# The first expert layer: one quad of tokens dense, three quads routed to their experts' blocks

## What is computed

```python
# layer 0: causal attention, 16 heads of 128, then
scores = sigmoid(x @ gate_w)                      # 32 experts
w, i = top_k(scores, 6); w /= w.sum() + 1e-20
g = einsum('td,edf->tef', x, wg); u = einsum('td,edf->tef', x, wu)   # 96 hidden values each
out = einsum('tef,efd,te->td', silu(g) * u, wd, combine(w, i)) \
      + (silu(x @ sg) * (x @ su)) @ sd            # shared: 192 hidden values
# layer 1: state-space layer (8 heads of 64, conv of 4 taps, dt = softplus, gated norm), then
# 16 experts of 176 hidden values, top 4 within 2 of 4 groups, and a shared part of 352
```

## Time and profile before

| | us |
|---|---|
| median of 3 runs | 1666.55 |
| lowest and highest run | 1663.94, 1666.93 |
| span of the profiled execution | 1664.1 |
| TensorE busy | 1607.4 |
| DVE, ACT, GpSimd busy | 1131.1, 764.6, 628.7 |
| bytes moved by DMA | 277.75 MB |

### The profile page before, as it was taken

The page is one execution under the profiler, slowest core; times in us unless marked ns, Lnnn a source line. Parts: engine busy times, 40 slices in busy tenths (PEclk is TensorE's granted clock), DMA queues, the critical chain, the costliest instruction groups (busy, mean ns, idle before and its releaser), DMA issues.

```text
span 1664.1 us, 29632 instructions
## 1 busy us (share of the span) xinstructions
PE 1607.4 (97%) x9944; PEld 1403.7 (84%) x9944; DVE 1131.1 (68%) x2877; ACT 764.6 (46%) x1889; POOL 628.7 (38%) x379
## 2 busy tenths in 40 slices
PE   7999999999999979999999999999999999999997
PEld 6988888898888868888888888888888888888886
DVE  5878878787887765556467568748784867753533
ACT  5666656666665543434433443325333533323221
POOL 2322223232222004323377335841575147533242
PEclk9999999999999999999999999999999999999999
DMA  6444335343443016666676556655655466555563
GB/s 212 159 140 143 141 118 180 132 158 139 142 141 137 1 59 205 191 196 205 199 225 188 184 176 209 194 187 165 207 189 175 146 206 197 178 175 172 195 206 107
DMA packets 101241, 277.75 MB, mean 167 GB/s; under 512 B 13488, under 2 KB 17584, under 8 KB 100112
## 3 DMA queue, kind: packets, MB, share of 16 engines
q1 hardware_dynamic: 101136, 276.39, 51.6%
HBM read 229.18 MB, written 46.63 MB: 166 GB/s over the span
## 4 chain that ended last, share of the span: by engine, by line
PE 60%; issue 14%; DVE 13%; POOL 6%; ACT 4%; DMA 1%; SPq 1%; POOLq 0%; DVEq 0%; ACTq 0%
PE psum L352 54%; POOL act_sb L578 4%; PE psum L1324 2%; DVE s_sb L1019 1%; PE psum L1335 1%; PE psum L1514 1%; POOL mix L600 1%; ACT p_sb L701 1%; PE psum L1314 1%; ACT kT_hi L660 1%; DVE s_sb L1017 1%; DVE kT_lo L913 1%; DVE pT_lo L1034 1%; DVE x L934 1%; DVE p_sb L1027 1%
## 5 line engine op out<-in xcount | busy, mean ns | idle before, releaser
L352 PE MATMUL psum<-xT_hi,gu_w 128*128 128x512 f32 x1616 | 550.3, 401 | 4.2 <-DVE act_sb L1082 4.0
L578 POOL TENSOR_TENSOR act_sb<-act_sb,comb 128x512 f32<-128x512 f32 x184 | 311.1, 1691 | 614.8 <-DVE act_sb L1082 614.6
L1082 DVE TENSOR_TENSOR act_sb<-psum,gated 128x512 f32<-128x512 f32 x204 | 140.7, 690 | 378.9 <-PE psum L352 372.6
L742 ACT ACTIVATE gated<-psum 128x512 f32<-128x512 f32 x204 | 122.2, 599 | 600.3 <-PE psum L352 597.8
L352 PEld LDWEIGHTS psum<-xT_hi,gu_w 128*128 128x128 f32 x1616 | 304.2, 188 | 78.0 <-DVE act_sb L1082 5.6
L352 PE MATMUL psum<-xT_lo,gu_w 128*128 128x512 f32 x808 | 319.6, 395 | 0.0
L352 PEld LDWEIGHTS psum<-d_w,act_hi 128*128 128x128 f32 x1632 | 221.5, 188 | 19.7 <-issue 2.1
L544 POOL TENSOR_TENSOR split_stage<-raw_stage,split_stage 128x768 fp32r<-128x768 f32 x56 | 103.1, 1840 | 354.2 <-ACT split_stage L650 354.2
L352 PE MATMUL psum<-d_w,act_hi 128*128 128x256 f32 x1632 | 227.7, 282 | 0.4 <-ACT act_hi L750 0.4
L352 PEld LDWEIGHTS psum<-xT_lo,gu_w 128*128 128x128 f32 x808 | 152.2, 188 | 28.8
L1088 DVE TENSOR_TENSOR act_lo<-act_sb,act_hi 128x512 fp32r<-128x512 f32 x204 | 148.8, 729 | 2.1 <-ACT act_hi L750 1.8
(11 more groups left out here) (203 smaller groups left out, 3473.6 us busy)
## 6 DMA issues: line engine op xcount, KB each, us to landing
gu_w<-w_split SPq DMA_DIRECT2D x204, 512.0 KB, 3.6
d_w<-w_split SPq DMA_DIRECT2D x204, 256.0 KB, 3.8
w_split<-split_stage SPq DMA_DIRECT2D x56, 768.0 KB, 3.9
raw_stage<-w_all SPq DMA_DIRECT2D x56, 384.0 KB, 4.3
decay_all<-decay_dram SPq DMA_DIRECT2D x32, 384.0 KB, 5.3
in_w<-w_split SPq DMA_DIRECT2D x40, 256.0 KB, 4.1
aw_raw<-attn_w SPq DMA_DIRECT2D x8, 1024.0 KB, 6.3
comb<-l_comb_dram SPq DMA_DIRECT2D x128, 64.0 KB, 3.1
```

The source lines that it names most:

```text
L352: last = nc.tensor.matmul(out_ap, w, m, start=start and n == 0, stop=stop and n == len(pairs) - 1, **kw)
L578: pool.tensor_tensor(act_sb[:, s % 2, :], act_sb[:, s % 2, :], comb[:, comb_block(s) % 2, :], ALU.mult).then_inc(comb_done, 1)
L742: act.activation(gated[to, s % 2, :], psum[0:to.stop - to.start, G_BANK, :], ACT.Silu).then_inc(gated_ready, 1)
L1082: dve.tensor_tensor(act_sb[r, s % 2, :], psum[r, G_BANK if packed(s) else U_BANK, :], gated[r, s % 2, :], ALU.mult).then_inc(t_ready, 1)
```

## The change

Layer 0 is dense for quad 0 alone. Quads 1 to 3 keep their two shared tiles, and each of their tokens goes to its six experts only.

- While quad 0 is computed, the gates of quads 1 to 3 are made (`choice_logits`, `choose`), a prefix sum by matmul gives each (token, choice) its row in its expert's region of `xs` in DRAM (`rank`, `rows_placed`), and GpSimd scatters the token rows there by indirect DMA: 36 units of two DMAs of 128 rows, one unit a tick, each after the one before has landed. `xs` is filled with zeros before, during attention (`zero`, 42 stores).
- A table gives the first row of each of 103 blocks of 128 rows (`table`, `rows_read`); SP reads these numbers into registers and loads, per block, the 128 rows and the weights of the block's expert (`rows_load`, `weights_load`).
- Then 103 block ticks: transposes, gate and up, SiLU, product, down, all in plain f32 without splitting, and a store to `os` for every second block.
- In layer 1's steps GpSimd gathers the six results of each token (36 units), and DVE adds them with their weights (`combine_rows`).
- All engines walk a list of ticks instead of steps: 32 dense ticks, 8 pauses, 103 blocks, 104 dense ticks. The 52 slots of a pair are mapped to ticks by `MARKS`: pair 0 lies over the blocks, pairs 1 to 3 lie in layer 1's steps, slots 0 to 44 in 9, 19 and 19 ticks, slots 44 to 52 in two.
- The norms of quads 1 and 2 move into the last attention group, that of quad 3 to tick 2.

```diff
+def tiles_of(f, q):
+    return f["lead"] if f is L0 and q else f["tiles"]
+STEP_LIST = [(f, q, j) for f in LAYERS for q in range(QUADS) for j in range(tiles_of(f, q))]
...
+SLOT = L0["experts"]
+TOP = L0["top"]
+WIDTH = L0["width"]
+BLOCK = 128
+BLOCK_BITS = 7
+REGION = ROUTED_TILES * P
+BLOCKS = (REGION * TOP + SLOT * (BLOCK - 1)) // BLOCK
+SPARE = BLOCKS - REGION * TOP // BLOCK
+LAST_ROW = SLOT * REGION + (SPARE - 1) * BLOCK
+UP = 2 * WIDTH
+BW = DC * UP + D
+ZERO_ROWS = 1280
+ZEROED = 6
+XS_ROWS = ZERO_ROWS * ZEROED * (GROUPS - 1)
+assert LAST_ROW + BLOCK <= XS_ROWS and BLOCKS <= P
+XB_RING, BW_RING, OUT_RING = 4, 6, 4
...
+Tick = namedtuple("Tick", "gate high down block")
+BREAK = first_step(L0, QUADS - 1)
+PAUSES = 8
+def dense_ticks(a, b):
+    at = lambda s: s if a <= s < b else None
+    return [Tick(at(s), at(s - 1), at(s - LAG), None) for s in range(a, b + LAG)]
+TICKS = dense_ticks(0, BREAK) + [Tick(None, None, None, None)] * PAUSES + [Tick(None, None, None, n) for n in range(BLOCKS)] \
+    + dense_ticks(BREAK, STEPS)
+B0 = BREAK + LAG + PAUSES
+K0 = B0 + BLOCKS
+def tick_of(s):
+    return s if s < BREAK else K0 + s - BREAK
+CHOICE = {1: 0, 2: 3, 3: 6}
+COUNTED = CHOICE[3] + 4
+WEIGHED = {1: 14, 2: 17, 3: 20}
+PAIRS_OF = QUAD * TOP // 2
+SCATTERED = 4
+UNITS_IN = 4
+GATHERED = [K0 + u for u in range(20)] + [K0 + 24 + u for u in range(4)] + [K0 + 29 + u for u in range(8)] + [K0 + 44 + u for u in range(4)]
+COMBINED = 3
...
+NORM = -6
+MARKS = (((NORM, 28), (0, 33), (4, 37), (8, 39), (9, B0 + 1), (52, B0 + 92)),
+         ((NORM, K0 + 15), (-3, K0 + 17), (0, K0 + 18), (44, K0 + 27), (52, K0 + 29)),
+         ((NORM, K0 + 30), (0, K0 + 33), (44, K0 + 52), (52, K0 + 54)),
+         ((NORM, K0 + 55), (0, K0 + 58), (44, K0 + 77), (52, K0 + 79)))
+SLOTS_AT = {}
+for _p in range(PAIRS):
+    for (_v, _n), (_w, _m) in zip(MARKS[_p], MARKS[_p][1:]):
+        for _s in range(_v, _w):
...
+            def zero(n):
+                by_part = xs.rearrange("(n p r) d -> n p (r d)", p=P, r=ZERO_ROWS // P)
+                dst = by_part[n] if isinstance(n, int) else by_part[bass.ds(n, 1)].rearrange("a p w -> p (a w)")
+                sp.dma_start(dst.rearrange("p (a w) -> p a w", w=BANK), zeros[:].to_broadcast([P, ZERO_ROWS // P * D // BANK, BANK])) \
+                    .then_inc(xs_zeroed, 16)
...
+            def weights_load(n):
+                row = first_row_of(n)
+                if n == 0:
+                    sp.wait_ge(down_done, BREAK)
+                wait(sp, b_down_done, n - BW_RING + 1)
+                sp.dma_start(block_w(n), l0_w[bass.ds(region_of(row), 1)].rearrange("a p w -> p (a w)")).then_inc(w_loaded[n % BW_RING], 16)
+            def rows_load(n):
+                row = first_row_of(n)
+                if n == 0:
+                    for q in ROUTED_QUADS:
+                        sp.wait_ge(scattered[q], 16 * QUAD * TOP)
+                wait(sp, xb_turned, n - XB_RING + 1)
+                sp.dma_start(xb[:, n % XB_RING, :], xs[bass.ds(row, BLOCK)]).then_inc(tokens_loaded[n % XB_RING], 16)
+            def block_store(n):
+                i, pair = n % 2, n // 2
+                if i == 0 and n < BLOCKS - 1:
+                    return
+                a = n - i
+                sp.wait_ge(b_copied, n + 1)
+                sp.dma_start(os[a * BLOCK:(n + 1) * BLOCK].rearrange("(i p) d -> p i d", p=P),
+                             b_out[:, 2 * (pair % 2):2 * (pair % 2) + i + 1, :]).then_inc(b_stored[pair % 2], 16)
...
+            for i, t in enumerate(TICKS):
+                s = t.gate
+                if t.block is not None:
+                    n = t.block
+                    if n + XB_RING < BLOCKS:
+                        rows_load(n + XB_RING)
+                    if n + BW_RING - 1 < BLOCKS:
+                        weights_load(n + BW_RING - 1)
+                    if n >= 1:
+                        block_store(n - 1)
+                if i == K0 - 1:
+                    gu_load(BREAK)
+                    gu_load(BREAK + 1)
+                    block_store(BLOCKS - 1)
...
+            def scatter(u):
+                q, v = ROUTED_QUADS[u // PAIRS_OF], u % PAIRS_OF
+                if u == 0:
+                    pool.wait_ge(xs_zeroed, 16 * ZEROED * (GROUPS - 1))
+                else:
+                    pool.wait_ge(scattered[ROUTED_QUADS[(u - 1) // PAIRS_OF]], 32 * ((u - 1) % PAIRS_OF + 1))
+                if v == 0:
+                    pool.wait_ge(placed, ROUTED_QUADS.index(q) + 1)
+                tile, ks = unit_rows(u)
+                for k in ks:
+                    pool.indirect_dma_start(xs, bass.IndirectOffsetOnAxis(ap=row_of[:, tile, k:k + 1], axis=0), x[:, FIRST_TILE + tile, :], None) \
+                        .then_inc(scattered[q], 16)
+            def gather(u):
+                if u == 0:
+                    blocks_stored(pool)
+                    pool.wait_ge(weighed, len(ROUTED_QUADS))
+                else:
+                    pool.wait_ge(og_loaded[(u - 1) % UNITS_IN], 32 * ((u - 1) // UNITS_IN + 1))
+                wait(pool, combined, u - UNITS_IN + 1)
+                tile, ks = unit_rows(u)
+                for j, k in enumerate(ks):
+                    pool.indirect_dma_start(og[:, u % UNITS_IN, j, :], None, os, bass.IndirectOffsetOnAxis(ap=back_of[:, tile, k:k + 1], axis=0)) \
+                        .then_inc(og_loaded[u % UNITS_IN], 16)
...
+            for i, t in enumerate(TICKS):
+                if t.gate is not None and not shared(t.gate):
+                    combine(t.gate)
+                if 0 <= i - SCATTERED < len(ROUTED_QUADS) * PAIRS_OF:
+                    scatter(i - SCATTERED)
+                if t.gate == 4:
                     ssm_constants()
-                if s == 9:
+                if t.gate == 9:
                     out_low()
-                for p in range(PAIRS):
-                    o = s - FRONT[p]
+                if i in GATHERED:
+                    gather(GATHERED.index(i))
...
+            def block_turned(n):
+                act.wait_ge(xb_turned, n + 1)
+                if n >= 2:
+                    act.wait_ge(gu_ready, n - 1)
+                act.activation(xbT[:, n % 2].rearrange("p c t -> p (c t)"), psum[:, TURN_BANK, 0:DC * BLOCK], ACT.Copy).then_inc(xbT_ready, 1)
+            def block_gate(n):
+                h = slice(0, WIDTH)
+                act.wait_ge(gu_ready, n + 1)
+                wait(act, bt_ready, n - 1)
+                act.activation(b_gated[h, n % 2, :], psum[h, gu_bank(n), 0:P], ACT.Silu).then_inc(b_gated_ready, 1)
+            def block_copy(n):
+                act.wait_ge(b_down_done, n + 1)
+                pair, i = n // 2, n % 2
+                if i == 0:
+                    wait(act, b_stored[pair % 2], 16 * (pair // 2))
+                act.activation(b_out[:, 2 * (pair % 2) + i, :], psum[:, DOWN_BANK, 0:D], ACT.Copy).then_inc(b_copied, 1)
...
+                    if norm and i in (12, 16):
+                        q = i // 4 - 2
+                        ln_stats(q, o_added, (GROUPS - 1) * 2 * PAIRS + 2 * q + 2)
+                        ln_root(q)
+                    if norm and i in (13, 17):
+                        ln_rows(0, i // 4 - 2)
...
+            def combine_rows(u):
+                tile, ks = unit_rows(u)
+                to = x[:, FIRST_TILE + tile, :]
+                dve.wait_ge(og_loaded[u % UNITS_IN], 32 * (u // UNITS_IN + 1))
+                for j, k in enumerate(ks):
+                    ins = dve.scalar_tensor_tensor(to, og[:, u % UNITS_IN, j, :], mix_of[:, tile, k:k + 1], to, ALU.mult, ALU.add)
+                    if j == 0:
+                        chained(ins)
+                ins.then_inc(combined, 1)
...
+            def block_act(n):
+                h = slice(0, WIDTH)
+                dve.wait_ge(b_gated_ready, n + 1)
+                wait(dve, b_down_done, n - 1)
+                dve.tensor_tensor(b_act[h, n % 2, :], psum[h, gu_bank(n), P:2 * P], b_gated[h, n % 2, :], ALU.mult).then_inc(bt_ready, 1)
...
+            def block_turn(n):
+                pe.wait_ge(tokens_loaded[n % XB_RING], 16 * (n // XB_RING) + 32)
+                wait(pe, xbT_ready, n)
+                for c in range(DC):
+                    last = pe.transpose(psum[:, TURN_BANK, c * BLOCK:(c + 1) * BLOCK], xb[:, n % XB_RING, c * P:(c + 1) * P], ident[:])
+                last.then_inc(xb_turned, 1)
+            def block_gate_up(n):
+                pe.wait_ge(xbT_ready, n + 1)
+                pe.wait_ge(w_loaded[n % BW_RING], w_landed(n % BW_RING, n, BREAK))
+                wait(pe, bt_ready, n - 1)
+                w, h = block_w(n), slice(0, WIDTH)
+                for i in range(2):
+                    last = chain(psum[h, gu_bank(n), i * P:(i + 1) * P],
+                                 [(w[:, c * UP + i * WIDTH:c * UP + (i + 1) * WIDTH], xbT[:, n % 2, c, :]) for c in range(DC)])
+                last.then_inc(gu_ready, 1)
+            def block_down(n):
```

(35 more changed lines are left out.)

579 lines of the change are left out of this document (414 added, 165 removed).

## The result

The changed kernel takes 1848.84 us (median of 4 runs, 1844.14 to 1851.56), the kernel before beside it 1665.24 us (4 runs, 1663.86 to 1666.93). The ratio is 1.1095, 95% interval 1.1074 to 1.1117. The forecast was 1692.5 us, with a range up to 1800: the direction was right, the size was not, and the result lies outside the range. The profiled execution's span is 1849.8 us, 185.7 us more than before.

The account below looks back on a forecast made before the run. TensorE, busy 97%, was taken to bound the kernel; its 127 us saved would be given back in waits. 620 + 188 + 227 + 643 + 12 = 1690, so 1692.5 us against 1666.55; range 1605 to 1800, the forecast's own 1650 to 1740.

Parts of the forecast that it names:

- Stage A: Attention and its tail: two more layer norms add 9 us, zero stores 0; dense steps start at 620 us.
- Stage B: Quad 0 dense while 72 indirect stores scatter: GpSimd sets the pace, 4.6 us a unit, 188 us in all.
- Rival 2: Indirect DMA costs a full GpSimd instruction, 6.5 us a unit in scatters, gather ticks +36: 1794 us; chance 0.12.
- Stage C: The 103 blocks: TensorE, DMA, SP and a load loop lie close together; 2.2 us a block, 227 us.
- Stage D: 102 dense steps with pairs 1 to 3 and 36 gathers: 429 + 135 + 70 + 5 + 4 = 643 us.
- rival 3: TensorE's clock drops to 1.2 GHz in the blocks' holes: a third of the stage 1750 us, all 1865; chance 0.08.
- The gathers: In layer 1's dense steps, gathers wait for each other: 4.6 against 4.23 us over 17 ticks without pairs, 5 us.
- Rival 1: Faster through shallower waits: scatter stage 167 us, blocks 206, chains beside the last dense steps 35; time 1615 us; chance 0.34.

Follow-up runs that it names:

- Experiment 7: Changed kernel, each scatter unit waiting for the unit two before it instead of the last one: 1799.67 us, ratio 1.0807.
- Experiment 9: Changed kernel, only the first quarter of a block's weights loaded from the seventh block on: 1820.42 us, ratio 1.0933.
- experiment 3: Kernel before with pairs 1 to 3 squeezed (19 steps), and from step 88 GpSimd's combine, ScalarE's high and DVE's low half behind the slots: 1751.91 us.
- experiment 4: Changed kernel, after the blocks GpSimd's combine behind the tick's slots: 1810.17 us; also ScalarE's high half and DVE's low half: 1791.53 us.
- experiment 2: Kernel before, slots 0 to 44 of pairs 1 to 3 in 33 steps: 1752.55 us; in 44 steps: 1684.35 us; last slots in two steps.
- Experiment 1: Kernel before, nothing routed, only pairs 1 to 3 squeezed: slots 0 to 44 in 19 steps, 44 to 52 in two: 1788.14 us, ratio 1.0724.
- experiment 8: Changed kernel, the 72 gathers replaced by GpSimd setting the tiles to a constant: 1819.97 us, ratio 1.0937.

## Why the prediction was right and wrong

**Stage A: right.** Dense steps were to start 9 us later; they start 8.2 later. The two more norms in the last group cost about what the rows said, and the zeros' stores cost nothing that shows.

**Stage B: a unit was sized at 4.6 us and took 5.1.** The issue was close (2 x 1.1 forecast, 0.97 + 0.30 + 0.97 measured). The multiply lies in the landing time, as forecast. What was mis-sized is the landing behind the second store: 2.4 us were left for it, and beside the dense work it was 3.3 at 700.87. Behind the dense ticks it was mostly 1.7, so the mean of 5.1 comes from 5.7 and 4.4. 36 units at 0.5 us and a start at 647 instead of 638 are the 28 us between the forecast's 188 and the 216 measured; why the first scatter started 9 us late was not looked into. Experiment 7 shows that the wait, and no work, set the pace. Rival 2, a dear issue, fell: the median is 0.97 us.

**Stage C: right.** 2.2 us a block and 227 us forecast, 2.19 and 226 measured. Experiment 9 adds which of the close limits it was: mostly TensorE (1.94 with few bytes), then the transfers, which ran at 323 GB/s with a share of 0.99 in the fullest window, a little under the 326 and 345 I had from the earlier trace rows.

**Stage D: the step that failed.** It holds 133 of the 160 us that the sum fell short. I took 79 us of waits (70 for the chains, 5, 4) and full clock: 643 us. It lasted 776. The windows give 161.7 us idle, 83 more than forecast, and 614.3 busy where I had 564, 50 more. Two things were wrong.
First, the waits. "Pairs 2 and 3 ... 14 us in the sums, I take 18" compared GpSimd's sum over a pair with TensorE's. That is the cost only if dense work and heads overlap freely, and the in-order queues of this kernel did not let them (experiments 3 and 4: 36 and 57 us by order alone; experiment 2: the cost begins between 44 and 33 steps a pair). TensorE's waits tell which terms were too small:

| TensorE's waits in stage D on | forecast, us | measured, us |
|---|---|---|
| `mix_lo` (the heads) | some 45 | 61.8 |
| `x` and `comb_tok` (norms and choices) | 5 + 3 + 4 + 4 = 16 | 30.9 + 19.8 = 50.7 |
| all else | 18 | 49.2 |

In pair 1's nine ticks the wait on `mix_lo` was 18.8 us, and 18 were forecast: chain less cover gave the right number there. In pairs 2 and 3 it was 23.8 and 19.2, where the sums left 10 each. The largest miss is the norms and choices, whose chains I let hide in pairs 2 and 3 but for 4 us each. Pair 1's nine ticks took 139.9 us, where the forecast had 117 for the whole pair (45, nine steps of 4.23, 34 of waits): 97.4 were busy, at a clock of 0.81, against 83, and 42.6 idle.
Of the squeeze's cost in the kernel before, order brings back 36 us. Of what stays, 29.5 us are longer busy time, and 57.7 are waits, 11.5 of them on `mix_lo` (experiment 3): the heads, serial on `mix_hi`, are a small part of it.
Second, the clock. I had it as rival 3, for stage C, where the holes looked many; there it stayed at 0.97 to 1.00. It fell to between 0.81 and 0.93 in the pairs, and to 0.87 in B. The row that spoke for it was in my hands: 0.83 in a window where TensorE was busy 7.6 of 10 us. It belonged to the stages whose waits I had forecast myself. Over the kernel TensorE's busy time fell by 50 us where 127 of work went: 77 us more than forecast. 50 of them are D's, and B's window holds 165.4 where I had 135. Experiment 1 shows 31.4 us of longer busy time for the pace alone, with the work unchanged.

**The gathers** were priced at 5 us, on 17 ticks without a pair; they cost 29, of which 13 lie in the 18 ticks ahead of pair 1 (experiment 8). In a pair's ticks they stand in GpSimd's queue too. An issue is 0.96 us in the median, and GpSimd waits 39.9 us for landings in all.

**The range** had its upper end from bounds of single terms. The bound of D's waits, 115 us (124 with the gathers and the start), was under the measured 161.7, because both ends used the same overlap. Rival 1 asked for that overlap to be better still. Its rows were about the scatters; for D's overlap no row spoke, and it took 0.34 of the chance.

What stays open: what each of the waits on `x`, `comb_tok` and the heads would give back if it alone were changed, what DVE's adding of the gathered rows costs there, and whether marks that keep pairs at one slot a step could make the change pay. That version, with a pair begun in the block stage, was not run.

## What to carry to other kernels

When steps are taken out of a schedule, look at the steps that remain and count how many pieces of side work each must now carry: with in-order queues on every engine a second piece was not averaged over its neighbours here, it added to its step. Put what waits for this step's TensorE work behind what is ready already, on every engine that carries both. And where you forecast TensorE's waits, forecast its granted clock for the same stage with them: equal matmuls took 31 us longer here where the engine kept being held up.

## What the runs showed of the hardware

- An indirect DMA of 128 rows of 1 KB takes GpSimd 0.97 us in the median (0.968 to 1.496) with 0.30 us to the next, against 0.33 and 0.35 for a plain issue on SP's queue. A chain of units of two, each awaiting the landing of the one before, took 5.1 us a unit (5.7 beside dense work, 3.96 at best); with the wait put one unit further back it took 3.9. The Trainium skill (SBUF — State Buffer, section "SBUF: two separate sides") says that GpSimd's descriptor writing is held off while DVE has the shared port. If that is the cause of the longest ones, it cost at most 0.53 us an issue here, and the median nothing. The longest, 1.50 us at 779.83, starts while DVE subtracts two SBUF tiles (`act_lo`, 779.79 to 780.48), which fits; no run separated it.
- Equal TensorE work took 1607.4, 1634.5 and 1638.8 us of busy time at mean clocks of 0.996, 0.978 and 0.975. The granted clock has two levels, 1.2 and 2.4 GHz, so 0.81 over pair 1's 140 us is, by an estimate from that row, some 53 us at the lower one (0.19/0.5 x 140). TensorE had come out of waits of up to 4.8 us on `mix_lo` and 6.6 on `x` there. Matmuls put ahead of the waits on `mix_lo` brought it to 0.87. In the block stage, where the waits after the first are short, it stayed at 0.98.
- GpSimd's multiply of 128 x 512 took 1.29 us at 700.90, where DVE stood idle from 701.62 on, and 1.67 at 1560.82 in the kernel before, where DVE's SBUF work went on beside it. The kernel before never showed less than 1.64: the forecast read its plain row as nearly free of the lock, and it was not.
